# A decoder layer: chunk 2 projected ahead of the attention, and chunk 0's cross attention between its steps

## The chip, the cores and the metric

The kernel runs on one core of a Trainium2 chip. The metric is the device time of one execution in microseconds. TensorE (PE) multiplies matrices, VectorE (DVE), ScalarE (ACT) and GpSimd (POOL) work on elements, and SyncE (SP) issues nearly all transfers. Each engine takes its instructions in the order in which they are written, and waits on semaphores for the others.

## The reference

The layer has three parts, each behind a layer norm and each added to x. Input x and the context are 16 blocks of 128 tokens with 256 channels.

```python
x = x + attn(layernorm(x), W_qkv, W_proj, b_proj, lambdas, subln_w)
x = x + xattn(layernorm(x), ctx_1024, ctx_1024, Wq, bq, Wk, bk, Wv, bv, Wf, bf)
x = x + ffn(layernorm(x), router_w, expert_bias, shared_w1, ..., routed_w3)
# attn, differential attention of 16 heads, head dimension 8 twice, values of 16:
o = softmax(q1 k1^T * scale) v - lam * softmax(q2 k2^T * scale) v
o = o * rsqrt(mean(o * o) + eps) * subln_w * (1 - lambda_init)      # for each head
return o @ W_proj + b_proj
# xattn: one head of 256 channels, temperature 8
attn = softmax((x Wq^T + bq) / 8 @ (ctx Wk^T + bk)^T)
return gelu((attn @ (ctx Wv^T + bv)) Wf^T + bf) + ctx
# ffn: a shared expert of 1024, and the best 2 of 16 routed experts of 256
```

## The kernel before

All data is float32, apart from the queries and keys, which are split into three bf16 parts each. The 16 blocks are handled as four chunks of four blocks (512 tokens), numbered 0 to 3.

**Opening.** For chunks 0 and 1 the core normalises x, turns it (`turn`, by matmuls with the identity), and multiplies it by the weights of queries and keys (`qk`, four products of 128x512 for a chunk, called f = 0 to 3) and of values (`values`, two halves). ScalarE writes the first bf16 part (`put_first`), VectorE subtracts it (`subtract_first`, which raises `rests`) and writes the second, GpSimd the third (`put_third`). SyncE stores the parts in memory (`store_part`, seven transfers of 256 KB for a chunk) and fetches them in the layout of the attention (`fetch`, twelve transfers of 128 KB for a unit). A unit is half the heads of a chunk, so there are eight, in three buffers (pack_q and pack_k).

**Attention.** It has 32 steps s, four for each unit; a step treats half the heads of one block of 128 tokens, in two halves a = 0 and 1. `scores(s, a)` on TensorE and `max_of` on VectorE find the maxima, three steps ahead (`LEAD = 3`); `split_max` (GpSimd), `turn_max` (TensorE), `copy_max` (ScalarE) and `put_max` (SyncE) bring them as extra rows to pack_q; `exps` and `exp` give the probabilities, `pv` weighs the values, `turn_o`, `invert` and `combine` finish. TensorE's order in a step is:

```python
for s in range(STEPS):
    exps(s, 0)
    if s + LEAD < STEPS: scores(s + LEAD, 0)
    if s: pv(s - 1, 1)
    between(s, 0)
    exps(s, 1)
    ...
```

**What stands between.** In `between` other work is put at places given by tables of steps. `TURN_AT` says where a chunk is turned, its four products follow in the next four steps; `VALUES_AT` is for values; `WEIGHTS_AT` for products of weights of the cross attention (`turn_wf`, `multiply_a`, `multiply_biases`, `multiply_m`); `CTX_AT` for a chunk of the context: turn, `project_keys` twice, `project_values` twice (U is its result); `OUT_AT` for `project_o`, the attention's output. On VectorE `sum_o`, `root_o` and `norm_o` normalise a chunk's heads in steps 11 and 12 for chunk 0, 19 and 20 for chunk 1, 27 and 28 for chunk 2, a chain of short instructions. Two PSUM banks, 6 and 7, serve all of this.

**Behind the steps.** A loop over the four chunks does the cross attention (`cross_scores`, `max_cross`, `exp_cross`, `turn_p`, `weigh_values`, `put_fo`, `gelu`, `add_cross`) and the first products of the shared expert (`up`, `down`) between. The routing, the scatter of rows to slots, 47 tiles of routed experts and the last chunk of the shared expert follow, and are not touched.

## Time and profile before

| what | us |
|---|---|
| median of 3 runs | 638.5 (636.83 to 640.86) |
| profiled execution | 641.78 |
| its span, first to last instruction | 640.5 |
| opening, to the first exponentials | 60.66 |
| 32 attention steps | 187.22 |
| behind the steps, chunk 0, 1 and 2 of the cross attention | 21.35, 24.92, 24.81 |
| TensorE busy in the span | 556.2 (87%) |

The span is the time between the first and the last instruction of the execution; the 1.3 us between it and the execution's time lie around it. The clock granted to TensorE had a mean of 0.937 of the full one.

### The profile page before, as it was taken

The numbers are of one execution on the slowest core, as the hardware profiler recorded it, in microseconds if no ns is written. First come the engines' busy times: TensorE is split into PE (matmuls) and PEld (weight loads), VectorE is DVE, ScalarE is ACT, GpSimd is POOL, SyncE is SP. The second block draws the span as 40 slices with busy tenths as digits, with TensorE's granted clock in tenths as the row PEclk, the third lists the DMA queues.
The fourth block names the chain that finished last, engine by engine and source line by source line (L and its number), as shares of the span: only waits on it lengthen the run. The fifth ranks groups of instructions, "written<-read, shape, count | busy, mean of one in ns | idle before, by whom it ended". The sixth has DMA issues, their size and how long they took to land.

```text
span 640.5 us, 9893 instructions
## 1 busy us (share of the span) xinstructions
PE 556.2 (87%) x3274; PEld 336.2 (53%) x3274; DVE 312.3 (49%) x677; ACT 227.2 (35%) x422; POOL 221.5 (35%) x449
## 2 busy tenths in 40 slices
PE   4933979859989979599999989997999999999995
PEld 2522435326555546565567537454566666655454
DVE  4634778884698754756415453210222223222263
ACT  6311564633735535346431410100333333332110
POOL 2421465655725434222101004663233433334000
PEclk9975897979989979799979999998999999999999
DMA  7697559436522329800006925222233223321711
GB/s 206 197 189 117 94 106 221 102 68 184 103 61 47 134 65 160 233 1 1 1 0 220 349 88 182 83 84 83 67 91 92 84 88 91 88 83 58 270 67 65
DMA packets 62144, 72.39 MB, mean 113 GB/s; under 512 B 14768, under 2 KB 55216, under 8 KB 60560
## 3 DMA queue, kind: packets, MB, share of 16 engines
q1 hardware_dynamic: 58304, 61.37, 38.9%
q0 software_dynamic: 3792, 10.39, 4.6%
q8 instruction: 29, 0.48, 0.3%
q14 instruction: 19, 0.16, 0.1%
HBM read 45.31 MB, written 26.03 MB: 111 GB/s over the span
## 4 chain that ended last, share of the span: by engine, by line
PE 38%; issue 19%; DVE 13%; DMA 12%; POOL 11%; ACT 5%; SPq 1%; POOLq 0%; DVEq 0%; ACTq 0%
PE ps L515 10%; DMA x_slots<-XN,slot_i 7%; POOL y_rows L1450 7%; PE ps L526 5%; PE ps L377 4%; PE ps L319 3%; PE ps L365 2%; ACT prob L1188 2%; DVE nmax L794 2%; PE ps L346 2%; PE ps L439 2%; PE ps L460 2%; PE ps L448 2%; DMA pack_k<-qk_parts 1%; PE ps L505 1%
## 5 line engine op out<-in xcount | busy, mean ns | idle before, releaser
L794 DVE TENSOR_REDUCE nmax<-ps 128x8 f32<-128x1024 f32 x64 | 77.8, 1216 | 51.6 <-PE ps L346 51.3
L570 PE MATMUL ps<-W,xt 128*128 x188 | 90.0, 602 | 0.7 <-ACT xt L1278 0.4
L1188 ACT ACTIVATE prob<-ps 128x1024 f32<-128x1024 f32 x64 | 65.4, 1022 | 34.2 <-PE ps L365 34.2
L1450 POOL DMA_INDIRECT y_rows<-yo,goes_to x47 | 45.8, 975 | 90.5 <-DVE yo L1001 90.5
L994 DVE TENSOR_TENSOR sa<-sa,ps 128x256 f32<-128x256 f32 x47 | 19.8, 421 | 97.7 <-ACT sa L1285 97.7
L515 PE MATMUL ps<-xT,W1s 128*128 128x512 f32 x128 | 62.1, 609 | 0.9 <-DVE yo L1001 0.9
L526 PE MATMUL ps<-W3s,hTs 128*128 128x256 f32 x256 | 58.7, 391 | 2.6 <-DVE hTs L927 2.6
L515 PE MATMUL ps<-xT,W2s 128*128 128x512 f32 x128 | 60.2, 592 | 0.0
L927 DVE TENSOR_TENSOR hTs<-sil,ps 128x512 f32<-128x512 f32 x32 | 22.0, 687 | 71.4 <-PE ps L515 59.5
L526 PEld LDWEIGHTS ps<-W3s,hTs 128*128 128x128 f32 x256 | 49.9, 196 | 12.1 <-DVE hTs L927 5.1
L1271 ACT ACTIVATE sil<-ps 128x512 f32<-128x512 f32 x32 | 19.1, 597 | 99.5 <-PE ps L515 78.8
L1535 POOL DMA_INDIRECT x_slots<-XN,slot_i x32 | 31.8, 992 | 60.0 <-DVE slot_i L977 39.9
L346 PE MATMUL ps<-pack_k,pack_q 48*128 48x128 bf16 x512 | 28.3, 235 | 24.6 <-DVE nmax L794 16.3
L377 PE MATMUL ps<-prob,Vp 128*32 128x256 f32 x512 | 45.8, 432 | 4.2 <-DVE OT L801 3.5
L590 PE MATMUL ps<-W,ht 128*128 x188 | 48.4, 381 | 0.4 <-ACT ht L1292 0.4
L570 PEld LDWEIGHTS ps<-W,xt 128*128 128x128 f32 x188 | 32.6, 193 | 24.7 <-issue 24.6
L1285 ACT ACTIVATE sa<-ps 128x256 f32<-128x256 f32 x47 | 18.0, 383 | 66.2 <-PE ps L570 66.2
L515 PEld LDWEIGHTS ps<-xT,W2s 128*128 128x128 f32 x128 | 24.3, 190 | 31.0 <-issue 29.7
L365 PEld LDWEIGHTS ps<-pack_q,pack_k 51*128 51x128 bf16 x512 | 15.8, 98 | 44.3 <-issue 36.8
L365 PE MATMUL ps<-pack_q,pack_k 51*128 51x128 bf16 x512 | 27.2, 229 | 13.3 <-ACT prob L1188 8.6
L515 PEld LDWEIGHTS ps<-xT,W1s 128*128 128x128 f32 x128 | 24.1, 195 | 26.1 <-issue 24.5
L1278 ACT ACTIVATE xt<-ps 128x256 f32<-128x256 f32 x47 | 18.0, 383 | 48.6 <-PE ps L560 48.6
(182 smaller groups left out, 868.9 us busy)
## 6 DMA issues: line engine op xcount, KB each, us to landing
W<-in_L_ffn_routed_w_dram SPq DMA_DIRECT2D x12, 1024.0 KB
qk_parts<-part SPq DMA_DIRECT2D x28, 256.0 KB, 3.7
pack_q<-qk_parts SPq DMA_DIRECT2D x48, 128.0 KB, 3.8
pack_k<-qk_parts SPq DMA_DIRECT2D x48, 128.0 KB, 4.3
xg<-x_slots SPq DMA_DIRECT2D x47, 129.0 KB
x_slots<-zero SPq DMA_DIRECT2D x11, 512.0 KB, 10.2
yg<-y_rows SPq DMA_DIRECT2D x4, 1024.0 KB, 8.5
X<-in_x_dram SPq DMA_DIRECT2D x4, 512.0 KB, 7.7
```

Source lines behind the costliest of these rows:

```text
L346: r = t.matmul(ps[:, m, h * P:(h + 1) * P], Qp[u][rr, 4 * a + h, lo:lo + P], Kp[u][rr, 4 * a + h, lo:lo + P], start=True, stop=True, tile_ ...
L365: r = t.matmul(ps[:, 2 + m, h * P:(h + 1) * P], Kp[u][rr, 4 * a + h, lo:lo + P], Qp[u][rr, 4 * a + h, lo:lo + P], start=True, stop=True, t ...
L377: r = t.matmul(ps[VP * h:VP * (h + 1), 4, a * 2 * P:(a + 1) * 2 * P], Vp[:, s // CS % 2, s % CB, s // CB % 2 * HU + 4 * a + h, :], prob[:, ...
L515: r = t.matmul(ps[:, i, :], w[:, k, f * P:(f + 1) * P], xT3[c][:, k, :], start=(k == 0), stop=(k == KT - 1))
L526: r = t.matmul(ps[:, 2 + j % 2, 0:D], hTs[:, f, j * P:(j + 1) * P], W3s[:, f, :], start=(f == 0), stop=(f == FS - 1))
L570: r = t.matmul(ps[:, 2 + p, :], xt[:, p, k, :], W12[:, ds(e, 1), k, :].rearrange("p o f -> p (o f)"), start=(k == 0), stop=(k == KT - 1))
L590: r = t.matmul(ps[:, 6 + p, 0:D], ht[:, p, k, :], W3[:, ds(e, 1), k, :].rearrange("p o f -> p (o f)"), start=(k == 0), stop=(k == KT - 1))
L794: v.tensor_reduce(nmax[:, s % 4, a, :, :], ps[:, 0:2, :].rearrange("p m (h t) -> p m h t", h=4), AX_X, ALU.max, negate=True).then_inc(maxe ...
L927: v.tensor_tensor(hTs[:, f, :], sil[:, f % 2, :], ps[:, 1, :], ALU.mult).then_inc(gated, 1)
L1188: a.activation(prob[:, n:n + 2, :], ps[:, 2:4, :], ACT.Exp, scale=HD ** -0.5).then_inc(exped, 1)
L1450: g.indirect_dma_start(out=y_rows, out_offset=bass.IndirectOffsetOnAxis(ap=goes_to[:, n:n + 1].bitcast(U32), axis=0), in_=yo[:, p, :], in_ ...
L1535: g.indirect_dma_start(out=x_slots, out_offset=bass.IndirectOffsetOnAxis(ap=slot_i[:, i, b:b + 1].bitcast(U32), axis=0), in_=XN[:, b, :], ...
```

## The change

- Chunk 2 is normalised, turned and multiplied by the weights of queries and keys in the opening, behind chunk 1, and kept turned in a tile of its own, `xT_2`. Its values stay in step 8. Before, its projection stood in steps 1 to 7.
- Chunk 3's projection begins in step 2 instead of step 9, the products of weights in step 9 instead of 14.
- The contexts' places move, each now by half steps (s, a); chunk 3's context, turned and projected to keys behind the steps before, is done in steps 25 and 26 (its U is left behind them).
- The rows of chunks 0 and 1 are normalised and turned for the cross attention in the steps (`ROWS_AT`), and chunk 0's whole cross attention stands in steps 19 to 22. The loop behind the steps begins at chunk 1. The normalisation of chunk 3's heads, which stood in the round of chunk 0 there, now stands in the round of chunk 1, and `project_o(3)` in that of chunk 2.
- In SyncE's queue, unit 1's fetches come in two halves behind `put_max(0)` and `put_max(1)`, where all stood ahead of both. Chunk 2's stores stand in steps 0 to 2. The stores have a semaphore for each chunk. The transfers that bring the contexts and the shared expert's weights keep their steps.

```diff
-TURN_AT = {2: 1, 3: 9}
+PROJECTED = 3
+TURN_AT = 2
 VALUES_AT = {2: 8, 3: 16}
-CTX_AT = {0: 17, 1: 22, 2: 27}
-OUT_AT = {0: 20, 1: 25, 2: 30}
-WEIGHTS_AT = 14
 LIFT_AT = 7
+WEIGHTS_AT = 9
+CTX_AT = {0: (11, 0), 1: (17, 0), 2: (23, 0), 3: (25, 1)}
...
@@ tensor: the opening
-            for c in range(2):
+            for c in range(PROJECTED):
                 turn(norm, c, 4, xn)
...
                 for f in range(4):
                     qk(c, f)
-                for i in range(2):
-                    values(c, i)
-
-
-            t.wait_ge(rests, 8)
+                if c < 2:
+                    for i in range(2):
+                        values(c, i)
+
+
+            t.wait_ge(rests, 4 * PROJECTED)
@@ tensor: behind the steps
             t.wait_ge(o_turned, STEPS)
-            turn(norm, NC, 4, xn)
-            turn_context(NC - 1, 0)
             t.wait_ge(x_added, 2 * (NC - 1))
-            for c in range(NC):
+            for c in range(1, NC):
                 cross_scores(c)
-                if c == 0:
-                    for e in range(KT):
-                        project_keys(NC - 1, e, 2 + e)
-                if c == 1:
+                if c == 2:
                     for i in range(2):
                         project_o(NC - 1, i, 4 + i)
@@ vector: between
+                if s == SCORES_AT[0]:
+                    max_cross(0)
+                if s == WEIGH_AT[0]:
+                    put_fo(0)
+                if s == WEIGH_AT[0] + 1:
+                    add_cross(0)
+                    v.wait_ge(x_done, 2)
+                    stats(norm3, 0, 0)
@@ vector: the opening
             split(1)
+            v.wait_ge(x_in[3], 16)
+            stats(norm, 3, 3)
+            split(2)
             prepare_weights()
@@ scalar
             def put_first(c, f):
                 a.wait_ge(qk_made, 4 * c + f + 1)
                 if c >= 2 and f == 0:
-                    a.wait_ge(parts_stored, 16 * STORES * c)
+                    a.wait_ge(parts_stored[(0, 2)[c - 2]], 16 * STORES)
@@ sync
             for i in range(3):
                 store_part(1, i)
-            fetch(1, range(PIECES))
             for s in range(LEAD - 1):
                 put_max(s)
+                fetch(1, range(3 * s, 3 * s + 3))
             for s in range(STEPS):
                 if s + LEAD - 1 < STEPS:
                     put_max(s + LEAD - 1)
-                for c, s0 in TURN_AT.items():
...
+                if s < 3:
+                    store_part(2, s)
```

The queue of SyncE in the opening, before. pack_q_76 and pack_k_79 are unit 0's buffers, pack_q_77 and pack_k_80 unit 1's, pack_q_78 unit 2's; mT holds the maxima.

```order
L1579 DMA pack_q_77<-qk_parts 16x4096 [waits parts_stored,k_ones]
L1579 DMA pack_q_77<-qk_parts 16x4096 x5
L1579 DMA pack_k_80<-qk_parts 16x4096 x6
L1587 DMA pack_q_76<-mT 3x8x128 [waits max_copied]
L1587 DMA pack_q_76<-mT 3x8x128
L1587 DMA pack_q_76<-mT 3x8x128 [waits max_copied]
L1587 DMA pack_q_76<-mT 3x8x128
L1587 DMA pack_q_76<-mT 3x8x128 [waits max_copied]
L1587 DMA pack_q_76<-mT 3x8x128
L1579 DMA pack_q_78<-qk_parts 16x4096 [waits parts_stored,k_ones]
```

The same place after; part_106 is chunk 2's parts, in the tile that chunk 0's had, and the third put_max is the first of the loop over the steps.

```order
L1621 DMA pack_q_76<-mT 3x8x128 [waits max_copied]
L1621 DMA pack_q_76<-mT 3x8x128
L1613 DMA pack_q_77<-qk_parts 16x4096 [waits parts_stored0,k_ones]
L1613 DMA pack_q_77<-qk_parts 16x4096 x5
L1621 DMA pack_q_76<-mT 3x8x128 [waits max_copied]
L1621 DMA pack_q_76<-mT 3x8x128
L1613 DMA pack_k_80<-qk_parts 16x4096 [waits parts_stored0,k_ones]
L1613 DMA pack_k_80<-qk_parts 16x4096 x5
L1621 DMA pack_q_76<-mT 3x8x128 [waits max_copied]
L1621 DMA pack_q_76<-mT 3x8x128
L1598 DMA qk_parts<-part_106 128x2x512 [waits firsts]
```

The fetches of unit 1 moved behind the first maxima, in halves, and the stores of chunk 2 stand ahead of unit 2's fetches.

ScalarE in step 22, before: the exponentials around the copies of the turned context.

```order
L1188 ACTIVATE prob<-ps 128x1024 [waits pv_done,s_done]
L1201 ACTIVATE cT<-ps 128x2x256 [waits ctx_turned] x2
L1188 ACTIVATE prob<-ps 128x1024 [waits pv_done,s_done]
L1181 ACTIVATE mT<-ps 128x128 [waits max_put0,max_turned]
L1209 ACTIVATE kT<-ps,kb_c 128x512 [waits keys_made]
```

ScalarE in step 22, after.

```order
L1215 ACTIVATE prob<-ps 128x1024 [waits pv_done,s_done]
L1241 ACTIVATE U<-ps 128x512 [waits o_normed,vals_made]
L1299 ACT_TABLE_LOAD
L1299 ACTIVATE fo<-fo 128x512 [waits fo_put]
L1299 ACTIVATE fo<-fo 128x512
L1215 ACT_TABLE_LOAD [waits pv_done]
L1215 ACTIVATE prob<-ps 128x1024 [waits s_done]
L1208 ACTIVATE mT<-ps 128x128 [waits max_put0,max_turned]
L1241 ACTIVATE U<-ps 128x512 [waits o_normed,vals_made]
```

Gelu of chunk 0 (fo) and two loads of tables now stand between the two exponentials of the step.

VectorE behind the last step's turn_o, before: chunk 2's output is added, then come chunk 0's maximum and the normalisation of chunk 3's heads (va).

```order
L805 RECIPROCAL rden<-OT 128x16 [waits o_turned]
L865 TENSOR_TENSOR X<-ps,X 128x512 [waits o_made,bp_added]
L865 TENSOR_TENSOR X<-ps,X 128x512 [waits o_made]
L896 TENSOR_REDUCE nm<-ps 128x4 [waits s_made]
L898 TENSOR_SCALAR nm<-nm 128x4 [waits vector_order]
L843 TENSOR_REDUCE va<-sq 128x64 [waits o_squared]
```

The same place after, where the first maximum is chunk 1's.

```order
L824 RECIPROCAL rden<-OT 128x16 [waits o_turned]
L921 TENSOR_REDUCE nm<-ps 128x4 [waits s_made]
L923 TENSOR_SCALAR nm<-nm 128x4 [waits vector_order]
L774 TENSOR_SCALAR XN<-X,mv_72,y_73 128x256 [waits ln_scaled3,combined]
L774 TENSOR_SCALAR XN<-X,mv_72,y_73 128x256 x3
L862 TENSOR_REDUCE va<-sq 128x64 [waits o_squared]
```

The sum of chunk 2 moved into step 31, and the third layer norm of chunk 0 (XN) came ahead of the head normalisation.

## Rows read from the trace of the kernel before

**Rows 1.** Windows: the steps, then chunks 0, 1 and 2 behind them.
```profile
core 0: us, PE busy (x) PEld busy (x) DVE busy (x) ACT busy (x) POOL busy (x), PEclk, DMA share, GB/s
60.66:247.88 187.22, 161.54 (x1775) 89.28 (x1775) 136.09 (x224) 95.99 (x142) 94.94 (x259) 0.91 0.52 103
247.88:269.23 21.35, 14.92 (x77) 11.42 (x77) 15.86 (x43) 10.84 (x24) 8.49 (x9) 0.85 1.04 278
269.23:294.15 24.92, 23.74 (x101) 16.67 (x102) 14.37 (x46) 12.96 (x23) 4.88 (x5) 0.92 0.00 1
294.15:318.96 24.81, 23.25 (x94) 14.16 (x93) 12.85 (x40) 12.63 (x24) 4.87 (x5) 0.93 0.00 1
```

**Rows 2.** Windows: steps 2, 6, 12-14, 20-22, 25, 28-31.
```profile
70.16:75.16 5.00, 4.57 (x53) 2.04 (x54) 3.47 (x5) 3.57 (x7) 2.36 (x8) 1.00 0.55 99
91.17:94.46 3.29, 2.72 (x49) 1.33 (x49) 2.73 (x5) 2.73 (x5) 1.54 (x6) 1.00 0.20 49
121.36:147.28 25.92, 17.63 (x168) 9.01 (x169) 19.77 (x33) 9.90 (x16) 16.09 (x34) 0.80 0.35 80
174.87:195.07 20.20, 17.79 (x183) 10.49 (x183) 18.95 (x37) 8.25 (x13) 6.97 (x24) 0.92 0.34 61
204.77:211.09 6.32, 6.32 (x67) 4.23 (x67) 3.46 (x5) 2.73 (x5) 4.12 (x13) 1.00 0.02 5
221.60:247.88 26.28, 21.17 (x192) 11.65 (x191) 12.40 (x29) 10.65 (x14) 7.31 (x22) 0.87 0.59 54
```

**Rows 3.** Chain of waits in the opening: start, us, what.
```profile
35.85 9.20 DMA pack_k<-qk_parts
...
53.26 7.35 DMA pack_q<-mT
```

**Rows 4.** Timeline of SyncE's queue in the opening.
```profile
40.26 6.20 SPq L1579 DMA_DIRECT2D pack_q<-qk_parts  x6
...
52.31 5.42 SPq L1587 DMA_DIRECT2D pack_q<-mT  x4
```

**Rows 5.** Timeline of the opening, TensorE and VectorE.
```profile
26.43 7.13 PE L319 MATMUL ps<-xT,Wqk 128*128 128x512 f32 x16 [0.79 <-ACT xT L1154]
...
33.40 3.62 PE L333 MATMUL ps<-Wv__93,xT 128*128 128x256 f32 x16
...
35.30 0.23 DVE L811 TENSOR_TENSOR lam<-lam 128x8 f32<-128x8 f32 x2
...
37.97 0.15 DVE L822 TENSOR_SCALAR neg_lam<-lw 128x1 f32<-128x1 f32 x1
...
47.84 1.22 DVE L794 TENSOR_REDUCE nmax<-ps 128x8 f32<-128x1024 f32 x1 [0.71 <-PE ps L346]
```

**Rows 6.** DMA issues: the stores, KB each, median us to landing.
```profile
qk_parts<-part SPq DMA_DIRECT2D x28, 256.0 KB, 3.7
```

**Rows 7.** Tile pack_k: from issue to landing.
```profile
DMA to landing us min/median/max: 3.0/4.3/12.0
```

**Rows 8.** Timeline of ScalarE around the start of step 2 (70.16).
```profile
69.91 0.27 ACT L1181 ACTIVATE mT<-ps 128x128 bf16<-128x128 bf16 x1
...
73.51 0.60 ACT L1162 ACTIVATE part<-ps 128x512 bf16<-128x512 f32 x1 [1.43 <-PE ps L319]
```

**Rows 9.** Timeline of ScalarE: a load of tables.
```profile
299.48 1.28 ACT L1271 ACT_TABLE_LOAD   x1
300.77 0.60 ACT L1271 ACTIVATE sil<-ps 128x512 f32<-128x512 f32 x1
```

**Rows 10.** Timeline behind the steps: head normalisation of chunk 3, TensorE in chunk 1.
```profile
253.28 1.21 DVE L843 TENSOR_REDUCE va<-sq 128x64 f32<-128x1024 f32 x1
...
259.40 1.25 DVE L857 STREAM_TRANSPOSE oT<-Ob 128x1024 f32<-128x1024 f32 x1
...
272.77 3.81 PE L460 MATMUL ps<-Wp,oT 128*128 128x256 f32 x16
...
281.08 1.96 PE L515 MATMUL ps<-xT,W1s 128*128 128x512 f32 x4
...
284.60 1.89 PE L549 MATMUL ps<-U,pT 128*128 128x256 f32 x8
```

More of the change, by code:

```diff
@@ L236, in decoder_layer @@
         qk_made, firsts, rests, seconds, thirds = (sem(n) for n in ("qk_made", "firsts", "rests", "seconds", "thirds"))
-        v_made, vt_put, parts_stored = sem("v_made"), sem("vt_put"), sem("parts_stored")
+        v_made, vt_put = sem("v_made"), sem("vt_put")
+        parts_stored = [sem(f"parts_stored{c}") for c in range(NC)]
         packed = [sem(f"packed{u}") for u in range(UNITS)]
@@ L867, in between @@
             def between(s):
-                for c, s0 in TURN_AT.items():
-                    if s == s0 - 1:
-                        normalize(norm, c, c, xn)
-                    if s0 < s <= s0 + 4:
-                        subtract_first(c, s - s0 - 1)
-                if s == TURN_AT[3] - 3:
-                    stats(norm, 3, 3)
+                if s == TURN_AT - 1:
+                    normalize(norm, 3, 3, xn)
+                if TURN_AT < s <= TURN_AT + 4:
+                    subtract_first(3, s - TURN_AT - 1)
                 if s == LIFT_AT:
@@ L884, in between @@
                         norm_o(c)
-                for c, s0 in OUT_AT.items():
-                    if c < 2 and s == s0 + 1:
+                for c, s0 in ADD_AT.items():
+                    if s == s0:
                         add_o(c, 6)
-                if s == OUT_AT[0] + 2:
-                    v.wait_ge(x_added, 2)
-                    stats(norm, NC, 0)
-                if s == OUT_AT[0] + 3:
-                    normalize(norm, NC, 0, xn)
+                for c, (s0, _) in ROWS_AT.items():
+                    if s == s0 - 2 + c:
+                        v.wait_ge(x_added, 2 * (c + 1))
+                        stats(norm, NC + c, c)
+                    if s == s0 - 1 + c:
+                        normalize(norm, NC + c, c, xn)
+                if s == SCORES_AT[0]:
[6 more added lines that the diff above has]
+                    stats(norm3, 0, 0)
             def max_cross(c):
@@ L1050, in vector_program @@
             invert(STEPS - 1)
-            add_o(2, 6)
-            for c in range(NC):
+            for c in range(1, NC):
                 max_cross(c)
-                if c == 0:
+                if c == 1:
+                    v.wait_ge(combined, STEPS)
+                    normalize(norm3, 0, 0, rows(XN, 0))
                     sum_o(NC - 1)
@@ L1217, in between @@
             def between(s, a_):
-                for c, s0 in TURN_AT.items():
-                    if (s, a_) == (s0, 1):
-                        put_turned(norm, c, 6, xT)
-                    if a_ == 0 and s0 < s <= s0 + 4:
-                        put_first(c, s - s0 - 1)
-                    if a_ == 0 and s0 < s - 1 <= s0 + 4:
-                        put_second(c, s - s0 - 2)
+                if (s, a_) == (TURN_AT, 1):
+                    put_turned(norm, 3, 6, xT)
+                if a_ == 0 and TURN_AT < s <= TURN_AT + 4:
+                    put_first(3, s - TURN_AT - 1)
+                if a_ == 0 and TURN_AT < s - 1 <= TURN_AT + 4:
+                    put_second(3, s - TURN_AT - 2)
                 for c, s0 in VALUES_AT.items():
@@ L1248, in between @@
                         square_o(c)
+                for c, place in ROWS_AT.items():
+                    if (s, a_) == place:
+                        put_turned(norm, NC + c, 6, xT, 1.0)
+                if (s, a_) == (SCORES_AT[0] + 1, 0):
+                    exp_cross(0)
+                if (s, a_) == TURN_P_AT:
+                    put_p(0)
+                if (s, a_) == (WEIGH_AT[0] + 1, 0):
+                    gelu(0)
             def exp_cross(c):
@@ L1299, in scalar_program @@
                 fill(Kp[u][:, :, :].rearrange("p h t -> p (h t)").bitcast(F32), TWO_ONES, k_ones)
-            for c in range(2):
-                put_turned(norm, c, 4, xT)
+            for c in range(PROJECTED):
+                put_turned(norm, c, 4, xT_of(c))
                 for f in range(4):
                     put_first(c, f)
-                for i in range(2):
-                    put_values(c, i)
+                if c < 2:
+                    for i in range(2):
+                        put_values(c, i)
             a.wait_ge(lam_summed, 1)
@@ L1458, in between @@
             def between(s):
[L1459 to L1463 removed]
+                if TURN_AT < s - 1 <= TURN_AT + 4:
+                    put_third(3, s - TURN_AT - 2)
                 for c in range(NC - 1):
@@ L1466, in between @@
                         clip_o(c)
-                if s == OUT_AT[0] + 2:
-                    scale(norm, NC)
+                for c, (s0, _) in ROWS_AT.items():
+                    if s == s0 - 2 + c:
+                        scale(norm, NC + c)
+                    if s == s0 + 1:
+                        add_context(c)
+                if s == WEIGH_AT[0] + 2:
+                    scale(norm3, 0)
                 if s in (11, 13, 16, 18):
@@ L1484, in gpsimd_program @@
                 put_third(1, f)
+            scale(norm, 3)
+            for f in range(4):
+                put_third(2, f)
             g.iota(spare[:, :, :], pattern=[[P, NT], [0, W - D]], base=2 * T + 1, channel_multiplier=1,
@@ L1503, in gpsimd_program @@
             clip_o(NC - 1)
-            add_context(0)
-            for c in range(NC):
+            for c in range(1, NC):
                 if c < NC - 1:
```

209 lines of the change are left out of this document (108 added, 101 removed).

## The prediction, made before the changed kernel had run

> **What bounds the kernel now.** I read the stage windows first, to see which stages the change can reach [rows 1]. The attention's 32 steps take 187.22 us with TensorE busy 161.54 and VectorE 136.09. Behind them stand 21.35 us for chunk 0's cross attention, in which TensorE is busy only 14.92 us, then 24.92 and 24.81 us for chunks 1 and 2, where TensorE is busy 23.7 and 23.3 us. So the piece after the steps is latency, and the two behind it are TensorE work.
>
> Second, the steps one by one [rows 2]. A step with nothing put between takes 3.29 us, one with one product of about 2 us 5.00, one with two 6.32: (6.32 - 3.29) / 2 = 1.5 us per product, since part of it fills waits. Three stretches are longer: in each, VectorE normalises the heads of a chunk (some 7.4 us in one piece) and TensorE waits for its maxima. They are steps 12 to 14 (25.92 us, clock 0.80), 20 to 22 (20.20) and 28 to 31 (26.28).
>
> Third, the opening. In the chain of waits two transfers end it: the fetch of unit 0 lands 9.2 us after its last issue, at 45.05, and the first maxima land 7.35 us after theirs, at 60.61 [rows 3]. The DMA queue shows why: the maxima are issued at 52.31, behind the twelve fetches of unit 1 that went out from 40.26 on [rows 4].
>
> **A. The opening up to the first exponentials: 0 us.** TensorE ends chunk 1's values at 37.0 [rows 5]. Turning chunk 2 adds 1 us and the copies 1.1; its four products take 7.1 us as chunk 1's did [rows 5], so they end at 46.2, and VectorE's last subtraction at 47.5. Then VectorE runs prepare_weights, 35.30 to 38.12 before, some 2.6 us, so the first maximum starts at 50.2 rather than 45.9. Maxima follow every 1.95 us (47.84 less the first one's 45.9). TensorE's own order puts six of them and two turned maxima ahead of exps(0), the fifth maximum ends at 59.2, exps(0) stands at 60.3. The first put_max goes out at 56.7 with an empty queue and lands by 60. Before it was 60.66, so what the later maxima cost, the moved put_max gives back. Bounds: -1 (TensorE warm between maxima) to +2.
>
> **B. Steps 0 to 3, new waits: +8.5 us.** Two.
> First, unit 1, which scores(4), in step 1, needs. Its first half is now queued behind put_max(0), 58.2 to 60.9, its second behind put_max(1), which waits for a turned maximum until about 61, so 62.4 to 65.1. Before, unit 1 was issued from 40.26 and the queue had run dry by 60.61. From 45.05, where unit 0 had landed, to 60.61 the queue worked off the rest of chunk 1's seven stores and unit 1's twelve fetches, 15.6 us [rows 3], so a unit keeps it busy for some 10 us. The median landing is 4.3 us behind the issue and the longest 12.0 [rows 7]. From 58.2 on I take 70 for the whole unit. Without the wait scores(4) would come at 64.5; 5.5 us late. Queued behind it on TensorE are pv(0), exps(1) and all of step 2. Bounds: 1 (landing at the median with no queue, and step 1 slack) to 10.
> Second, part 0's buffer. put_first(3,0) waits on ScalarE for all seven stores of chunk 2. The last two are issued behind put_max(4), which waits for copy_max in step 2; in the trace this copy stands at 69.91, 0.25 us before the next step [rows 8, 2]. Put_max takes 1.5 us and the stores 1.0, so they are out 2.3 us into step 3 and land at 6.0 with the median of 3.7 [rows 6]. put_first is wanted 3.35 us into its step (73.51 less 70.16) [rows 8, 2]: 2.6 us for ScalarE, and exp(3,1) and TensorE's exps(4) are queued behind it. With 0.5 us for put_max behind 1.25 MB of stores and fetches a step: +3. Bounds: 0 to 8.
> The Trainium skill (DMA: Bandwidth & Descriptors, Queues, rings and completion order) says that each DMA engine takes descriptors in ring order. The 7.35 us for two small rows of maxima agree [rows 3]. It speaks against this change too: put_max(1) now stands behind half of unit 1 and put_max(2) to (4) behind stores and fetches; a rule without a number changes no term.
>
> **C. The other attention steps: +3.4 us.** Counted in products of 2 us, the steps outside the three stretches held 21 and hold 22, and 4 turnings of 128 tokens by four and now 8 (chunk 3's contexts, two chunks' rows, Wf): 1 x 1.5 + 4 x 1.0 = +5.5 us. What is taken out is chunk 2's four products (steps 2 to 5) and its turning; what is put in are chunk 3's keys, one cross score and one weighing.
> Steps 12 to 14: the projection of chunk 3 no longer meets the head normalisation of chunk 0, and turn_wf with multiply_a no longer the cold clock behind it. Three bare steps and four products make 3 x 3.29 + 4 x 1.5 = 16. What the stretch took beyond that was 10 us before; in steps 20 to 22, without a projection, it was 20.20 - 16.6 = 3.6. I take 6 between the two, since POOL's add_bias stays in step 13: 22, so -3.9.
> Steps 20 to 22: VectorE gets put_fo, add_cross and stats beside the normalisation. It needs some 3.5 us a step for two maxima (1.22 each [rows 5]), turn_o and invert, so 10.5 + 6.2 (the normalisation without sum_o) + 5 (1.9, 1.3 and 1.8, estimates) = 22; ScalarE gets gelu with two table loads in step 22. I take 23.5, so +3.3. Behind step 22's loads exp(22,1) is queued, and TensorE waits for it in step 23. One load takes 1.28 us [rows 9]: 2.6 for two and 1.2 for gelu, on 2.73 us of ScalarE's work in step 25 [rows 2] and 0.6 for a second copy of U, make 7.1 against a step of 6.32. The Trainium skill (ScalarE: Activation LUTs, What ACT_TABLE_LOAD costs) gives 2.66 us for a switch, with a drain. The trace shows none: the load at 299.48 ends at 300.76 and silu starts at 300.77 [rows 9]. By the page two switches would cost 2.8 us more.
> Steps 28 to 31: four products for five, and the same stall: -1.5.
> Sum 5.5 - 3.9 + 3.3 - 1.5 = 3.4. Bounds -5 (the stretches 12 to 14 and 28 to 31 lose their stalls) to +9 (VectorE's 15.86 us in the old stage for chunk 0, less the 7.4 that stay there, all on the path) [rows 1].
>
> **D. Behind the steps: -15.1 us.** Before, from the last step to chunk 3's scores: 21.35 + 24.92 + 24.81 = 71.08. After, count from the last step. Cross scores of chunk 1 end at 2.0, its maximum at 3.1, then VectorE runs normalize(norm3, 0), 1.4, and only then the head normalisation of chunk 3, 253.28 to 260.65 before, 7.4 [rows 10]: it ends at 11.9. ScalarE's two copies of U, 1.1, end at 13.1, and TensorE's up(0, 0) waits for them. Up takes 3.5 us and weigh_values follows (281.08 and 284.60) [rows 10], so the weighing starts at 16.9; from there to the next scores it is 294.15 - 284.60 = 9.55, so 26.5, and with 0.2 for gate_up in its way, 26.7. Chunk 2's round gets project_o(3), 3.6 us at the full clock for its 16 passes (as many as values in rows 5; at 272.77 they took 3.81 [rows 10]), and 0.9 until add_o lets TensorE on: 24.81 + 4.5 = 29.3. Together 56.0, so -15.1. project_keys(3), turn_context(3) and add_o(2) went with C. Bounds: -19 (chunk 1's round becomes as short as one of TensorE work alone) to -11 (the clock falls as it did after 21.35 us of gaps, 0.85 [rows 1], and doubles 4 us of work). All behind, the router, the scatter and the routed experts, hangs on this chain, and moves as a whole.
>
> **Nothing in "loaded sooner".** The four context loads stay in steps 3, 7, 11 and 15, and the shared experts' weights in 25 to 29; what comes sooner is their use. I cost it at 0: the context of chunk 0 is loaded at step 3 and turned at step 11.
>
> **Sum.** 0 + 8.5 + 3.4 - 15.1 = -3.2 us. The profiled execution has 641.78 us (span 640.5), 3.3 above the median of 638.5. So 638.6 for it, and 635 against the median. A measurement tells about 1% (6.4 us) from no change.
>
> **Rivals.**
> 1. The opening doesn't stall. Unit 1's second half lands at the median 4.3 us after issue and the stores of chunk 2 before put_first asks. For it: windows with half a megabyte a step show the DMA engines at a share of 0.55 [rows 2]. Against: 1 to 1.25 MB a step is twice that. B falls to 2, which gives 628.8.
> 2. Slower: the opening's queue backs up. The mechanism is one: put_max, unit 1, unit 2 and chunk 2's stores share a queue that takes 1 to 1.25 MB a step for three steps, with 1.5 MB of unit 1 ahead. For it: the longest landing of 12.0 us [rows 7], and the SP issue of six fetches that took 6.20 us at 40.26 [rows 4]. It decides when the backlog exceeds the two steps by which put_max leads, some 9 us; then every exps of steps 2 to 5 waits, and B rises by 12 to 20: 647.
> 3. The gain behind the steps is half eaten, since chunk 3's head normalisation now stands in chunk 1's round and the clock falls: D is -11, which gives 639.
>
> **Chances.** Forecast 0.45 (by itself 630 to 641), rival 1 0.25, rival 2 0.2, rival 3 0.1. The range has to reach rival 1 and C's lower bound, and most of rival 2: 624 to 646. Faster by over 1% (below 632.1) are rival 1 and a part of the forecast, 0.35; slower by over 1% (above 644.9) rival 2, 0.2; the rest 0.45.
>
> **What would show it.** A: the first exponentials at 60 to 61. B: TensorE idle 4 to 6 us in step 1 until pack_k lands, and ScalarE idle before put_first in step 3. C: steps 12 to 14 near 22, 20 to 22 near 23.5. D: chunk 3's scores 56 us behind the last step. I am wrong if maxima are waited for in every early step, or if the steps shrink below 185 us with the waits taken out.

## The result, and the profile after

| | before | changed |
|---|---|---|
| median, us | 639.68 (636.83 to 642.33, 4 executions) | 654.01 (650.49 to 660.3, 4 executions) |
| profiled execution, its span | 641.78, 640.5 | 650.49, 649.2 |

The changed kernel is slower: ratio 1.0194, 95% interval 1.0143 to 1.0244. Here and below ratios leave disturbed executions out, and they are not the quotient of the medians. The forecast was 635, range 624 to 646. The two profiled executions lie 8.7 us apart, less than the medians' 14.3: 641.78 is near the top of the times before, and 650.49 is the lowest of the changed kernel.

Windows of the changed kernel: the 32 steps, the rounds of chunks 1 and 2 behind them, all behind those, then steps 0 to 7, 12 to 14, 17, 20 to 22 and 28 to 31.
```profile
core 0: us, PE busy (x) PEld busy (x) DVE busy (x) ACT busy (x) POOL busy (x), PEclk, DMA share, GB/s
58.79:273.16 214.37, 167.84 (x1811) 93.77 (x1810) 145.78 (x240) 101.42 (x154) 97.29 (x263) 0.89 0.50 97
273.16:300.98 27.82, 24.02 (x100) 15.61 (x101) 18.47 (x55) 13.67 (x25) 6.18 (x8) 0.94 0.79 215
300.98:327.36 26.38, 25.30 (x110) 16.30 (x109) 14.34 (x42) 12.74 (x24) 4.88 (x5) 1.00 0.00 1
327.36:649.20 321.84, 303.24 (x1103) 186.69 (x1101) 103.36 (x249) 76.26 (x188) 91.38 (x138) 0.97 0.35 111
...
58.79:108.25 49.46, 33.82 (x411) 15.87 (x410) 29.67 (x39) 22.98 (x35) 19.40 (x60) 0.81 0.69 137
133.27:156.09 22.82, 18.47 (x178) 10.63 (x177) 16.43 (x29) 8.94 (x13) 11.20 (x30) 0.85 0.34 72
167.21:176.90 9.69, 7.00 (x62) 3.14 (x62) 4.94 (x12) 3.79 (x6) 7.91 (x16) 0.83 0.45 85
188.02:212.06 24.04, 15.68 (x176) 9.19 (x176) 21.86 (x44) 12.92 (x24) 9.52 (x29) 0.93 0.27 47
245.57:273.16 27.59, 21.07 (x187) 11.77 (x186) 15.56 (x29) 10.04 (x13) 9.18 (x21) 0.82 0.53 49
```
Against [rows 1] the account closes: the opening -1.87 (58.79 for 60.66), the steps +27.15 (214.37 for 187.22), chunk 1 and 2 behind them -16.88 (54.20 for 71.08), the rest +0.30: +8.70. So in this execution what was to be gained behind the steps was gained, and the steps gave back more. TensorE is busy only 6.3 us longer in them, so for some 21 of the 27 us it stands idle.

Timeline of the changed kernel at those waits; the brackets say how long an engine stood idle and for whom.
```profile
65.39 0.61 PE L376 MATMUL ps<-pack_q,pack_k 51*128 51x128 bf16 x8 [1.57 <-DMA pack_q<-mT]
...
70.62 0.61 PE L357 MATMUL ps<-pack_k,pack_q 48*128 48x128 bf16 x8 [4.62 <-DMA pack_k<-qk_parts]
...
85.69 0.60 ACT L1189 ACTIVATE part<-ps 128x512 bf16<-128x512 f32 x1 [5.50 <-DMA qk_parts<-part]
...
87.34 0.40 PE L376 MATMUL ps<-pack_q,pack_k 51*128 51x128 bf16 x8 [3.83 <-ACT prob L1215]
...
88.56 3.54 PE L331 MATMUL ps<-xT,Wqk 128*128 128x512 f32 x4
...
168.02 1.04 POOL L1422 TENSOR_TENSOR y<-y,minus_half 128x4 f32<-128x4 f32 x1
...
169.03 2.35 POOL L1425 TENSOR_TENSOR X<-X,bp_b 128x1024 f32<-128x1024 f32 x1
...
172.67 0.23 PE L365 MATMUL ps<-identb,mpart 128*128 128x128 bf16 x1 [2.69 <-POOL mpart L1445]
...
173.40 3.57 PE L451 MATMUL ps<-cT,A_T 128*128 128x512 f32 x4
...
207.14 1.28 ACT L1299 ACT_TABLE_LOAD   x1
...
209.60 1.28 ACT L1215 ACT_TABLE_LOAD   x1
210.90 1.02 ACT L1215 ACTIVATE prob<-ps 128x1024 f32<-128x1024 f32 x1
...
212.06 0.40 PE L376 MATMUL ps<-pack_q,pack_k 51*128 51x128 bf16 x8 [2.37 <-ACT prob L1215]
...
229.94 1.06 PE L444 MATMUL ps<-ident,Cx 128*128 128x128 f32 x8 [1.88 <-DVE X L884]
...
243.70 1.94 PE L320 MATMUL ps<-ident,xn 128*128 128x128 f32 x8 [2.46 <-DVE xn L774]
...
250.59 2.35 POOL L1486 TENSOR_TENSOR X<-X,Cx 128x1024 f32<-128x1024 f32 x1
...
250.71 2.28 DVE L786 TENSOR_SCALAR yo__56<-yo__56 128x64 int32<-128x64 int32 x1
...
258.87 1.03 PE L388 MATMUL ps<-prob,Vp 128*32 128x256 f32 x8 [4.64 <-DVE OT L820]
...
259.83 3.25 PE L466 MATMUL ps<-M_T,cT 128*128 128x256 f32 x8
```
Step 1 begins with a wait for its maxima, and in it scores(4) waits for unit 1; in step 3 put_first(3,0) waits for chunk 2's stores, and TensorE for ScalarE. In step 17 GpSimd runs scale and add_bias(2) ahead of split_max, and turn_max waits. At the start of step 23 exps waits for the exp that stood behind the two table loads. In 25 and 27 the turnings of the context and of chunk 1's rows wait for VectorE's work of the same step. In 28 and 29 VectorE's root_o stands beside GpSimd's add_context(1), and one of its 128x64 instructions takes 2.28 us. After such idle time the granted clock is down (0.81 to 0.85 in four of these windows), and the next product (four matmuls of 512 columns or eight of 256) takes 3.3 to 3.6 us and not 2.0. The chain of waits names the two transfers too:
```profile
63.91 6.66 DMA pack_k<-qk_parts
...
80.80 4.81 DMA qk_parts<-part
```

### The profile page after: what moved, and what is told of

Read it like the earlier page. It is cut to its first block, busy times and chain, and to the rows that moved or that the text cites. A ratio compares the mean times of both kernels' runs of the same rounds, so it can differ in the third digit from the quotient of the medians.

```text
span 649.2 us, 9894 instructions
## 1 busy us (share of the span) xinstructions
PE 558.6 (86%) x3274; PEld 333.9 (51%) x3274; DVE 319.1 (49%) x681; ACT 225.9 (35%) x418; POOL 221.8 (34%) x449
## 4 chain that ended last, share of the span: by engine, by line
PE 40%; issue 19%; DVE 13%; DMA 10%; POOL 10%; ACT 5%; SPq 2%; POOLq 0%; DVEq 0%; ACTq 0%
PE ps L543 12%; DMA x_slots<-XN,slot_i 7%; POOL y_rows L1480 7%; PE ps L331 5%; PE ps L554 5%; PE ps L388 3%; PE ps L451 3%; DVE nmax L813 3%; PE ps L480 2%; PE ps L376 2%; ACT prob L1215 2%; PE ps L344 2%; PE ps L357 2%; PE ps L466 1%; POOL goes_to L1474 1%
## 5 line engine op out<-in xcount | busy, mean ns | idle before, releaser
L543 PE MATMUL ps<-xT,W1s 128*128 128x512 f32 x128 | 64.0, 625 | 3.1 <-ACT U L1241 1.6
L554 PEld LDWEIGHTS ps<-W3s,hTs 128*128 128x128 f32 x256 | 49.6, 195 | 11.9 <-DVE hTs L952 5.1
L1452 POOL TENSOR_SCALAR rden<-rden,neg_lam 128x8 f32<-128x8 f32 x32 | 9.8, 307 | 92.8 <-DVE rden L824 92.7
L376 PE MATMUL ps<-pack_q,pack_k 51*128 51x128 bf16 x512 | 27.8, 233 | 15.7 <-ACT prob L1215 14.1
```

The source lines that it names most:

```text
L376: r = t.matmul(ps[:, 2 + m, h * P:(h + 1) * P], Kp[u][rr, 4 * a + h, lo:lo + P], Qp[u][rr, 4 * a + h, lo:lo + P], start=True, stop=True, t ...
L543: r = t.matmul(ps[:, i, :], w[:, k, f * P:(f + 1) * P], xT3[c][:, k, :], start=(k == 0), stop=(k == KT - 1))
L554: r = t.matmul(ps[:, 2 + j % 2, 0:D], hTs[:, f, j * P:(j + 1) * P], W3s[:, f, :], start=(f == 0), stop=(f == FS - 1))
```

## The experiments

Where nothing else is said, time in steps is read from TensorE's first exps of each step in the profiled execution. Many such step times repeat to a few hundredths of a microsecond from kernel to kernel, but not all. Steps 23 to 27 take 33.51 us in the changed kernel and in e2, 35.07 in e3 and e6 and 36.62 in e1, and steps 20 to 22 take 23.9 to 25.5, though none of these edits stands there. In these two stretches a difference of under 3 us says nothing by itself. By stretches of steps, in us:

```
                  0-7   8-11  12-14  15-19  20-22  23-27  28-30
before           39.11  21.59  25.92  27.59  20.20  26.53  20.46
changed          49.46  25.02  22.82  31.93  24.04  33.51  23.08
e1_fetch_whole   45.33  25.04  21.63  33.19  23.85  36.62  23.69
e2_stores_step0  47.81  26.23  23.02  31.92  24.02  33.51  23.07
e3_both          46.50  24.79  22.42  31.95  25.22  35.07  23.09
e4_before_split  47.72  21.63  25.92  27.60  20.22  26.53  20.46
e5_gpsimd        49.64  25.03  22.82  27.78  25.63  34.97  20.84
e6_turn3         41.15  23.74  22.65  31.95  25.49  35.07  23.07
e7_all           41.50  23.74  22.61  27.76  24.03  31.72  21.35
e8_chain         42.49  23.37  21.40  27.56  25.25  31.13  20.02
e11_clear        41.37  23.38  17.81  31.52  19.39  30.92  18.45
p1_projection    37.89  22.03  24.27  27.60  21.50  26.53  21.13
e9_before_chain  38.46  23.00  23.97  27.81  19.24  29.41  15.12
e10_p1_chain     38.35  22.03  24.92  28.47  20.67  29.45  15.13
```

**The opening's queue: e1, e2, e3.** Three edits of the changed kernel's order on SyncE: the fetch of unit 1 whole and first (e1), the seven stores of chunk 2 all in step 0 (e2), both (e3).
```
+            fetch(1, range(PIECES))             # e1, e3
             for s in range(LEAD - 1):
                 put_max(s)
-                fetch(1, range(3 * s, 3 * s + 3))
...
-                if s < 3:                       # e2, e3
-                    store_part(2, s)
+                if s == 0:
+                    for i in range(3):
+                        store_part(2, i)
```


> The changed kernel, with all twelve fetches of unit 1 issued ahead of both maxima, as the kernel before had them. Theory of the queue's order: the wait for pack_k in step 1 (4.62 us) and most of step 0's excess go, exps(0) comes back from 58.8 to some 60.7, steps 0 and 1 fall from 15.6 to 8 us, so some 5 us are gained against the changed kernel. Rival, that the DMA engines' bytes are the limit of the first steps whatever the order: the wait reappears at put_max or the stores, and the time stays within 1 us of the changed kernel's. The wait for chunk 2's stores in step 3 stays in both.

> The changed kernel, with chunk 2's seven stores all issued in step 0 instead of three, two and two in steps 0 to 2. Theory of the queue's order: the stores land before put_first(3,0) wants part 0's buffer, ScalarE's wait of 5.50 us and TensorE's of 3.83 in step 3 go, step 3 falls from 8.8 to some 5.3, and 3 to 4 us are gained. Rival, bytes: 1.75 MB ahead of put_max(3) make exps(3) wait as long as the stores did, and the time doesn't move.

> Both edits of the queue together on the changed kernel. Theory of the order: steps 0 to 4 take 24 us instead of 35.5, exps(0) at 60.7 instead of 58.8, so some 9 us gained against the changed kernel, about 642 to 645, still not under the kernel before, since the later steps lost some 11 us more than forecast. Rival, bytes: under 3 us.

e1: 647.11 us, ratio 1.0089 (1.0048 to 1.013). The wait for pack_k is gone, steps 0 to 4 take 31.39 us for 35.52, and the first exponentials come no later (58.94). e2: 650.45, 1.0128 (1.0053 to 1.0204); step 3 falls from 8.79 to 6.49, and the interval still overlaps that of the changed kernel. e3: 651.12, 1.0155 (1.0083 to 1.0227), no better than either alone, within what its rival allowed (under 3 us), and steps 0 to 4 take 32.23, more than in e1. Its timeline shows why:
```profile
77.47 0.61 PE L376 MATMUL ps<-pack_q,pack_k 51*128 51x128 bf16 x8 [5.54 <-DMA pack_q<-mT]
```
The maxima of step 3 now stand behind the stores. So order alone helps only as far as the transfer moved isn't put ahead of one that is wanted sooner.

**One half of the change alone: p1.** The kernel before with chunk 2 projected in the opening and nothing else; chunk 3 stays at step 9, the cross attention behind the steps.
```
-TURN_AT = {2: 1, 3: 9}
+PROJECTED = 3
+TURN_AT = {3: 9}
```


> One part alone: the kernel before, with chunk 2 projected in the opening and its stores in steps 0 to 2; everything else keeps its place, so the cross attention of chunk 0 stays behind the steps, chunk 3 is projected at step 9, and unit 1's fetches stay ahead of the maxima. If the early projection is good by itself: exps(0) some 3 us later than 60.7 (the later first maximum, with put_max behind the fetches as before), steps 1 to 5 shorter by 1.5 to 2 us each, so the time falls by 4 to 7 us below the kernel before. If the opening is where the change loses whatever the queue's order, it is slower by 5 us or more.

637.62 us against 642.52 before, 0.9932 (0.9896 to 0.9968). This half is a gain, if a small one, of the size that was expected but not in the expected place: the first exponentials came at 58.17 and not some 3 us after 60.7, and steps 1 to 5 shrank by 2.4 us together, where 1.5 to 2 each were expected. It has the fetch of unit 1 ahead of put_max, and its chunk 3 asks for the stores only in step 10.

**Does the split fetch cost by itself? e4, on the kernel before.**
```
-            fetch(1, range(PIECES))
             for s in range(LEAD - 1):
                 put_max(s)
+                fetch(1, range(3 * s, 3 * s + 3))
```


> The kernel before with one edit: the fetch of unit 1 is not issued whole ahead of the first two put_max, but in halves behind each of them, as the changed kernel does. Theory (the order on SyncE's queue costs by itself): steps 0 to 2 grow by the wait for pack_k of scores(4), 4 to 5 us as in the changed kernel (4.62), so 4 to 5 us slower, a ratio of 1.006 to 1.008. Rival (the wait arises only because the changed kernel's opening leaves the queue fuller): the kernel before has slack there, under 1 us slower, 0.999 to 1.002.

646.92 against 640.11, 1.0083 (1.0047 to 1.012): it does, by the upper end of what was expected. Timeline of e4, steps 0 and 1:
```profile
63.42 0.61 PE L365 MATMUL ps<-pack_q,pack_k 51*128 51x128 bf16 x8 [2.45 <-DMA pack_q<-mT]
...
69.04 0.61 PE L346 MATMUL ps<-pack_k,pack_q 48*128 48x128 bf16 x8 [5.01 <-DMA pack_k<-qk_parts]
```
Steps 0 to 3 take 28.5 us for 19.9. Against that the first exponentials come at 55.94 and wait for no maxima, since put_max(0) has no fetch of unit 1 ahead of it. From the first scores (45.28, and 45.19 before) to the end of step 3 it is 39.2 us for 35.3. How far before's own opening can be leaned on, e9 below tells: it has the opening of before, word for word, and its first exponentials came at 56.42 and not 60.66, since unit 0 landed 2 us sooner and the wait for the maxima was 2.64 us and not 4.74.

**GpSimd's order: e5, on the changed kernel.**
```
-                    if s == s0 + 1:
+                    if c == 0 and s == s0 + 1:      # add_context(1): behind the steps
-                if s in (11, 13, 16, 18):           # add_bias
+                if s in (11, 13, 21, 24):
```


> The changed kernel with GpSimd's large additions moved: add_bias of chunks 2 and 3 from steps 16 and 18 to steps 21 and 24, and add_context of chunk 1 from step 28 to behind the steps. No other engine's order changes. Theory (GpSimd's order is what the sum missed): step 17 falls from 9.69 to 5.5 to 6.5 us, since split_max no longer stands behind scale and add_bias; steps 28 to 31 fall from 27.59 to about 25; step 24 or 21 rises by at most 1. In all 4 to 6 us less than the changed kernel, a ratio to the kernel before of 1.010 to 1.014. Rival (steps are long because TensorE's own work in them is more than 1.5 us a product, and its clock falls in them): step 17 stays above 8.5 and the sum of the steps within 2 us, ratio 1.017 to 1.021.

647.9 us, 1.0126 (1.0054 to 1.0198), 6 us below the changed kernel by the medians, as expected; the intervals overlap, and it is the two steps aimed at that show the effect. Step 17 falls from 9.69 to 5.59 and step 29 from 13.24 to 10.99, with the work on TensorE the same. Step 22 rises by 2.2 and 23 by 1.5, but that can't be put down to add_bias(2) at step 21: with the addition where it was, e3 shows 1.3 and 1.6, and e6 1.4 and 1.6.

**When chunk 3 is projected: e6, e1 and one number more.**
```
-TURN_AT = 2
+TURN_AT = 3
```


> The changed kernel with the fetch of unit 1 whole ahead of the put_max (as e1_fetch_whole) and with TURN_AT = 3, so that every piece of chunk 3's projection comes one step later. Theory (the store wait in step 3 is a matter of when put_first(3,0) comes, as the stores land about 5.5 us behind it): steps 0 to 4 take 3 to 5 us less than in e1_fetch_whole (31.4 there), 26.5 to 28.5, with no wait in their place; ratio 1.000 to 1.006. Rival (bytes: whatever order is chosen, the queue's backlog of the opening has to drain before the steps run freely): a wait of like size turns up at put_max or at a later fetch, steps 0 to 5 within 1.5 us of those of e1_fetch_whole, ratio 1.007 to 1.013.

644.91, 1.0086 (1.0049 to 1.0124). In the steps it does what was expected: 0 to 4 take 25.15 us for 31.39, and no like wait turns up. In the whole it is only 2.2 us below e1, its ratio lies in the range given to the rival, and the intervals don't tell e6 from e1; so the steps speak for the theory, the total for neither. Of the 6.2 us in steps 0 to 4 two come back since the last product moves to step 7: steps 0 to 7 hold the same work in both and take 41.15 for 45.33, 4.2 less. Against the changed kernel that is 8.3 us, the price of its transfer waits.

**All waits together: e7**, e6 with e5's moves and two placements.
```
-CTX_AT  ... 3: (25, 1)          KEYS_AT ... 3: ((26, 0), (26, 1))
+CTX_AT  ... 3: (26, 0)          KEYS_AT ... 3: ((26, 1), (27, 0))
-                    if s == s0 - 2 + c:   # stats, scale;  normalize at s0 - 1 + c
+                    if s == s0 - 2:       #                normalize at s0 - 1
```


> All of it together: fetch of unit 1 whole, TURN_AT = 3, GpSimd's additions moved as in e5_gpsimd, and two placements: statistics and normalization of chunk 1's rows in steps 25 and 26 (they were in 26 and 27, where the turn of (27,1) waits for them), the context of chunk 3 at (26,0) with keys at (26,1) and (27,0) (it was at (25,1), where it waits for add_o of the same step). Theory (the loss is a sum of waits that have nothing to do with the amount of work): e1 gave 7 us, the store wait 3 to 4, GpSimd 4 to 6, the placements 3 to 4; from 654 that makes 632 to 637, a ratio of 0.987 to 0.997. Rival (the steps are full, work put in them costs what it would cost behind them): not below 643, ratio 1.003 or more.

635.29 against 640.11, 0.9929 (0.9889 to 0.9968): 18.7 us below the changed kernel by the medians, with the same instructions. The rival, that work put into full steps costs what it costs behind them, falls. What remains stands in three places. In steps 12 to 14:
```profile
135.14 1.19 DVE L813 TENSOR_REDUCE nmax<-ps 128x8 f32<-128x1024 f32 x1
...
136.38 0.40 PE L357 MATMUL ps<-pack_k,pack_q 48*128 48x128 bf16 x8 [3.70 <-DVE nmax L813]
...
140.08 3.73 PE L466 MATMUL ps<-M_T,cT 128*128 128x256 f32 x8
```
VectorE had run root_o and norm_o from 129.19 to 135.2 in one piece. In step 26 (9.76) GpSimd's scale waited for VectorE's statistics ahead of split_max. Steps 28 and 29 are as 12 and 13.

**VectorE's chain: e8, e9, e10.** One edit on e7, on before and on p1 (in e8 also scale one step later).
```
-                    if s == CS * c + 11:     +                    if s == CS * c + 10:
                         sum_o(c)
-                    if s == CS * c + 12:     +                    if s == CS * c + 11:
                         root_o()
+                    if s == CS * c + 12:
                         norm_o(c)
 # clip_o: CS * c + 9 -> 8; square_o: (CS * c + 10, 1) -> (CS * c + 9, 1)
```


> e7_all with VectorE's chain of each chunk's norm spread over three steps where it stood in two: clip_o, square_o and sum_o one step earlier, root_o one step earlier (11, 19, 27), norm_o where it was (12, 20, 28); and GpSimd's scale of the normalized rows one step later (17 and 26), behind that step's split_max and combine, so that no split_max stands behind a wait for VectorE's statistics. Theory (in steps 12, 20 and 28 VectorE works 6.0 us in a row, so max_of, turn_o and with them TensorE stop for about 4 us, and TensorE's clock is low for the next 5 to 8 us): steps 12 to 14, now 22.6 us, fall to 17 to 19; 20 to 22, now 24.0, to 20 to 22; 28 and 29, now 15.7, to 10 to 12; step 26 from 9.76 to 6 to 7; steps 11, 19 and 27 rise by up to 1 each. In all 10 to 14 us less than e7_all: 621 to 626, a ratio of 0.970 to 0.980. Rival (VectorE's work there has to be done in some step, and wherever it stands the step grows by it): under 3 us less, ratio above 0.987.

> The kernel before with the same spreading of VectorE's chain alone (clip_o, square_o, sum_o and root_o one step earlier, norm_o where it was). Theory: the stall is in the kernel before as well, so most of the gain is to be had without the change studied here: steps 12 to 14 fall from 25.9 to 17 to 19 us, 20 to 22 from 20.2 to 18 to 19, 28 to 30 from 20.5 to 16 to 18, 11, 19 and 27 rise by up to 1 each: 8 to 12 us less, a ratio of 0.981 to 0.988. Rival as for e8_chain: under 3 us, 0.995 to 1.000.

> p1_projection (the kernel before with only the third chunk's projection moved into the opening) with the same spreading of VectorE's chain. If the two gains add: 0.9932 less 1.2 to 1.9 per cent, 0.974 to 0.981. Beside e8_chain it tells whether the first chunk's cross attention between the steps is worth anything once the waits are gone: if e8_chain is lower by over 0.4 per cent, it is; if the two are alike or e8_chain is higher, the projection alone carries the gain.

e8: 631.79 against 643.29, 0.9826 (0.9788 to 0.9863). e9: 636.47, 0.9906 (0.9872 to 0.994). e10: 638.1, 0.9913 (0.9883 to 0.9944). All three missed their ranges. By the ratios e8 is some 6.6 us below e7, where 10 to 14 were expected, and e9 some 6 below before, where 8 to 12 were. On p1 the edit shows no gain clear of noise (0.9913 to 0.9932): steps 28 to 30 fall by 6.0 us, but 23 to 27 rise by 2.9 and others with them. The stall had moved: in e9 steps 12 to 14 fall by 2 us only, since step 12 rises from 5.44 to 9.80. Its timeline:
```profile
119.60 2.34 POOL L1396 TENSOR_TENSOR X<-X,bp_b 128x1024 f32<-128x1024 f32 x1
119.73 2.27 DVE L766 TENSOR_SCALAR yo__56<-yo__56 128x64 int32<-128x64 int32 x1
...
125.91 0.61 PE L346 MATMUL ps<-pack_k,pack_q 48*128 48x128 bf16 x8 [4.58 <-DVE nmax L794]
```
root_o in step 11 had come beside add_bias(0), and one instruction waited for the whole of it, as at 250.71 in the changed kernel. e10 has the same pair there (2.27 us), and e8 in steps 11 and 19.

**That pair taken apart: e11**, e8 with add_bias(0) in step 9 and add_context(0) in step 18.
```
-                if s in (11, 13, 21, 24):
+                if s in (9, 13, 21, 24):
-                    if c == 0 and s == s0 + 1:
+                    if c == 0 and s == s0:
```


> e8_chain with two of GpSimd's whole-chunk additions (2.35 us each) taken out from beside VectorE's chain root_o: add_bias of chunk 0 from step 11 to 9, add_context of chunk 0 from step 19 to 18. The same instructions, none more, none less. Theory (VectorE is held for as long as GpSimd's addition of three whole SBUF tiles runs: one 128x64 instruction that takes 0.20 us by itself took 2.28 beside it in e8_chain, in step 11 and in step 19): root_o is 2.1 us shorter each time; step 12 falls from 6.86 to 4.7 to 5.5, steps 13 and 14 together from 14.54 to 11 to 13.5 since TensorE's idle time and low clock go with it, step 20 from 9.26 to 6 to 7; steps 9 and 18 rise by up to 1. In all 5 to 8 us less than e8_chain: 624 to 627, a ratio of 0.971 to 0.975. Rival (the long instruction marks a wait that would be there anyhow): root_o keeps a long instruction somewhere and the time stays within 1.5 us of e8_chain, 0.980 to 0.985.

627.51 us against 642.08, 0.9758 (0.9696 to 0.982): 4.3 us below e8 by the medians where 5 to 8 were expected, with intervals that overlap; it is faster than before, and no other kernel here has a lower median. Timeline and windows of e11 (the instruction that was held; the steps and the two rounds behind):
```profile
123.09 0.20 DVE L786 TENSOR_SCALAR yo__56<-yo__56 128x64 int32<-128x64 int32 x1
```
```profile
58.95:246.30 187.35, 162.88 (x1812) 92.65 (x1811) 141.66 (x240) 101.24 (x154) 97.70 (x262) 0.93 0.51 102
246.30:274.11 27.81, 24.02 (x100) 15.63 (x101) 20.48 (x55) 13.67 (x25) 8.49 (x9) 0.94 1.01 223
274.11:300.49 26.38, 25.30 (x110) 16.28 (x109) 14.34 (x42) 12.74 (x24) 4.88 (x5) 1.00 0.00 1
```
Step 12 falls to 4.89 and steps 12 to 14 to 17.81. Not all went as expected: step 20 falls from 9.26 to 4.30 but step 19 rises from 5.55 to 9.51. Its timeline shows the same pair once more, with another instruction of VectorE:
```profile
163.82 2.35 POOL L1487 TENSOR_TENSOR X<-X,Cx 128x1024 f32<-128x1024 f32 x1
...
164.30 1.92 DVE L865 TENSOR_SCALAR fits<-va 128x64 f32<-128x64 f32 x1
...
167.55 0.61 PE L357 MATMUL ps<-pack_k,pack_q 48*128 48x128 bf16 x8 [1.91 <-DVE nmax L813]
...
169.32 3.78 PE L563 MATMUL ps<-kT,xT 128*128 128x128 f32 x16
```
The instruction fits<-va of sum_o, 0.20 us where no addition runs (at 118.59), was held for 1.92 us by add_context(0), now in 18, and the maximum behind it came late. split_max stood behind the addition too, and cross_scores(0) met a low clock (3.78 us for its 16 passes, 2.05 in the changed kernel). So the addition was moved from one short instruction of VectorE to another, and e11 isn't the end of what order can give. The steps take 187.35 us, what they took before [rows 1], with the first chunk's cross attention in them.

## Why the prediction was wrong

**C, the other attention steps, is the step that failed: +3.4 forecast, +18.9 measured, far outside its bounds of -5 to +9.** It is the 27.15 of the steps less the 8.3 of B. The profiled executions explain 11.9 of the 19 us between 635 and 654.01 (650.49 against the 638.6 forecast for it), and C's excess of 15.5, less what A and D gained, is all of that. The rest lies between profiled executions and medians, on both sides.

The stretches were near: 12 to 14 took 22.82 (22 forecast), 20 to 22 took 24.04 (23.5), the two table loads 1.28 each with exp right behind them, and TensorE waited for it in step 23, as assumed; 28 to 31 took 27.59 where 24.8 were forecast. What failed was "1 x 1.5 + 4 x 1.0 = +5.5" for the ordinary steps: they took 16.8 more (139.92 less 8.3, against 114.8 before). The count itself holds: the matmuls in these steps are one product and some four turnings more, as counted. Windows of the steps 8 to 11 and 23 to 27, before and changed:
```profile
99.77:121.36 21.59, 19.98 (x232) 11.13 (x229) 17.32 (x29) 13.01 (x20) 13.30 (x38) 0.94 0.85 177
195.07:221.60 26.53, 25.12 (x294) 14.70 (x294) 20.39 (x34) 15.02 (x22) 14.60 (x46) 1.00 0.36 103
...
108.25:133.27 25.02, 23.45 (x260) 14.63 (x257) 17.83 (x27) 13.12 (x20) 13.78 (x38) 1.00 0.83 171
212.06:245.57 33.51, 27.66 (x302) 15.46 (x303) 22.44 (x41) 17.32 (x27) 15.21 (x45) 0.95 0.29 82
```
In all ordinary steps TensorE is busy 7.7 us more than before, and idle 17.4 us more, of which B is 8.3 (the sums of these windows over the four ordinary stretches). What the prediction put at nothing is the rest of the idle time: a count of TensorE's products prices a step in which nobody else is late. By stretches:
- Steps 8 to 11, +3.4: busy time is up by 3.5, so this is work that came in from later steps, and no wait.
- Step 17, +4.3: scale and add_bias(2) ahead of split_max. e5 moved the addition and the step fell to 5.59. The prediction named add_bias in step 13, where it had been seen, and didn't look where scale would now meet it.
- Steps 23 to 27, +7.0: busy time is up by 2.5, the rest is idle. The waits at 229.94 and 243.70 are shown. Whether taking them out gave anything is not: e7 is 1.8 lower here and e11 2.6, less than this stretch varies without an edit.
- Steps 28 to 31, one of the stretches, 2.8 above forecast: of it 2.2 went with add_context(1) in e5.
- With those waits gone, in e7, the ordinary steps still take 9.9 more than before, not 5.5: TensorE is busy 6.3 us more and idle 3.6 more, and steps 23 to 27 hold 5.2 of the 9.9. Part is step 26's wait for scale; the rest I haven't taken apart.

That order and not the amount of work made the steps long is shown by e7 and e11: with the same instructions, but for add_context(1), which stands behind them, they take 197.21 and 187.35 us for 214.37. Which wait costs how much is shown for steps 0 to 7, 17 and 29, and open for the rest.

**B, the new waits of steps 0 to 3: right in places, order and size.** Forecast 5.5 + 3 = 8.5; e1 gave 4.1 us in steps 0 to 7, e6 another 4.2, together 8.3 (by the medians 9.1 in the whole). The first was a little smaller, the second larger. Unit 1 had landed at 70.57, where 70 was forecast, and chunk 2's last stores 7.1 us into step 3, where 6.0 was. Rival 2 didn't come: its 12 to 20 us, with every exps of steps 2 to 5 waiting, are in no trace. Its mechanism, maxima stuck behind bulk transfers, did, once for 5.54 us, in e3, and for 1.57 and 2.45 us at step 1 in the changed kernel and e4.

**A, the opening: 0 forecast, -1.9 read.** That is just outside its bounds of -1 to +2, and nothing to lean on: the opening of before, word for word, gave 60.66 and 56.42. The first maximum began at 49.07, 1.1 sooner than worked out. The moved put_max gave nothing back: in e1, with the fetches ahead of it, the first exponentials came at 58.94 without a wait.

**D, behind the steps: -15.1 forecast, -16.9 measured**, 54.20 us for the 56.0 that were worked out. That it came so near is in part luck. Chunk 1's round took 27.8 for 26.7 and chunk 2's 26.4 for 29.3, two errors that cancel. (Its sum slips by 0.3: 13.1 and 3.5 are 16.6, not 16.9; the weighing began at 18.3.) And TensorE had the full clock in chunk 2's round here, so rival 3 didn't come, but in e1, e2 and e7 the two rounds took 58.5 to 58.6 us, in e1 and e7 at a clock of 0.83 and 0.94. There D is -12.5, near rival 3's -11.

**Rival 1** (no stall in the opening) is what p1 shows for the first half of the change, and it is a gain of 0.7%. No rival held that other engines' order in the later steps would cost more than the steps behind gave; that is the case that came.

**Is the second half of the change worth its place?** With the waits in, no: changed against p1 is 1.0194 to 0.9932. With e7's waits out it costs and gives nothing: 0.9929 to 0.9932. With VectorE's chain spread as well it seems so: e8 is at 0.9826 and e10, p1 with the same chain, at 0.9913, more than the 0.4% set beforehand, though the intervals almost touch and e8 has GpSimd's moves as well. p1 with these moves wasn't run, so how much of e11's 2.4% needs the cross attention in the steps stays open.

## What to carry to other kernels

Where work is put between the steps of a pipelined loop, price it on each engine in its own order, not by the busiest engine's count: for every step, what stands ahead of the short instruction that the next step waits for (here split_max on GpSimd, max_of on VectorE, put_max on the queue). In a queue that transfers share, order them by when each is wanted, and not by size: small maxima put ahead of unit 1's fetches made those late (e4), and stores put ahead of maxima made these late (e3). Where a store is late for its buffer, asking for the buffer one step later (e6) did more than storing sooner (e2, e3). When a change of order loses, its waits can be taken out one by one with the same instructions: here they were worth 4% from the changed kernel to e11. And price a stretch from more than one profiled execution where it varies without an edit, as steps 23 to 27 and the rounds behind do here.
